# Moving old-key probabilities of all four row tiles, and one chunk of new keys, through square transposes and DRAM in a gated attention block

## The reference, cut to what matters

```
x = layernorm(x)                       # 4 x 512 x 512
q = x @ wq.T ; k_new = x @ wk.T ; v_new = x @ wv.T
k = concat([ctx, k_new])               # 1024 keys
v = concat([ctx, v_new])
attn = softmax(q @ k.T / sqrt(512))    # 512 x 1024 a batch
out = (attn @ v) @ wo.T
x = x + tanh(g_xattn) * out
x = x + tanh(g_ffn) * relu(layernorm(x) @ sign(up).T * up_scale) @ sign(down).T * down_scale * output_scale
```

## Time and profile before

| | us |
|---|---|
| median of 3 runs | 582.67 |
| the profiled execution | 583.08 |
| span of its instructions | 581.1 |
| TensorE busy in it | 575.6 |
| VectorE, ScalarE, GpSimd busy | 392.0, 280.6, 117.8 |

### The profile page before, as it was taken

The page is one execution under the profiler, slowest core; times in us unless marked ns, Lnnn a source line. Parts: engine busy times, 40 slices in busy tenths (PEclk is TensorE's granted clock), DMA queues, the critical chain, the costliest instruction groups (busy, mean ns, idle before and its releaser), DMA issues.

```text
span 581.1 us, 6945 instructions
## 1 busy us (share of the span) xinstructions
PE 575.6 (99%) x2642; PEld 478.5 (82%) x2642; DVE 392.0 (67%) x552; ACT 280.6 (48%) x406; POOL 117.8 (20%) x111
## 2 busy tenths in 40 slices
PE   9999999999999999999999999999999999999997
PEld 7888888888888888888888888888888888888885
DVE  5889554587675587673587676777569644766654
ACT  3783522473322463322475455656458345555531
POOL 5006403003003003003002015242422012332002
PEclk9999999999999999999999999999999999999999
DMA  8714432024115055115124613283821311230011
GB/s 288 241 70 138 81 108 73 18 70 130 38 46 99 16 202 145 38 50 97 33 76 109 216 49 133 74 180 109 177 78 37 144 32 42 95 123 37 0 73 72
DMA packets 76352, 55.78 MB, mean 96 GB/s; under 512 B 54944, under 2 KB 59040, under 8 KB 75936
## 3 DMA queue, kind: packets, MB, share of 16 engines
q1 hardware_dynamic: 76320, 55.34, 32.4%
HBM read 42.74 MB, written 12.60 MB: 95 GB/s over the span
## 4 chain that ended last, share of the span: by engine, by line
PE 98%; DVE 1%; ACT 0%; issue 0%
PE proj L673 36%; PE score L791 19%; PE turn L776 12%; PE score L706 9%; PE score L673 7%; PE proj L776 5%; PE proj L706 4%; PE score L916 2%; PE turn L665 1%; PE score L665 1%; PE score L923 1%; DVE rows L1775 1%; DVE scaled L1772 0%; ACT four_x L1008 0%; PE proj L665 0%; ACT weights L1000 0%
## 5 line engine op out<-in xcount | busy, mean ns | idle before, releaser
L791 PE MATMUL score<-down_signs,hid_split 128*128 128x512 f32 x512 | 133.4, 389 | 0.0
L791 PEld LDWEIGHTS score<-down_signs,hid_split 128*128 128x128 f32 x512 | 96.0, 188 | 20.3 <-DVE hid_split L1656 0.5
L673 PE MATMUL proj<-probsT,four_x 128*128 128x512 f32 x384 | 88.1, 390 | 0.0
L673 PEld LDWEIGHTS proj<-probsT,four_x 128*128 128x128 f32 x384 | 71.8, 188 | 14.7
L673 PE MATMUL proj<-four_x,weights 128*128 128x512 f32 x336 | 76.8, 389 | 0.0
L673 PEld LDWEIGHTS proj<-four_x,weights 128*128 128x128 f32 x336 | 63.0, 188 | 13.0
L597 POOL TENSOR_TENSOR four_x<-raw_ctx,four_x 128x2048 fp32r<-128x2048 f32 x7 | 32.6, 4656 | 147.9 <-ACT four_x L1004 147.9
L1656 DVE TENSOR_TENSOR hid_split<-hid,hid_split 128x512 fp32r<-128x512 f32 x64 | 44.3, 695 | 15.5 <-ACT hid_split L1218 15.4
L776 PE MATMUL turn<-ops_b,up_ops 128*128 128x512 f32 x192 | 51.3, 389 | 0.0
L1012 ACT ACTIVATE four_x<-proj 128x512 fp32r<-128x512 f32 x32 | 19.0, 593 | 65.4 <-PE proj L673 65.4
L1218 ACT ACTIVATE hid_split<-hid 128x512 fp32r<-128x512 f32 x64 | 40.0, 630 | 20.9 <-PE score L791 18.1
(11 more groups left out here) (136 smaller groups left out, 861.1 us busy)
## 6 DMA issues: line engine op xcount, KB each, us to landing
raw_w<-in_ffn_w SPq DMA_DIRECT2D x21, 512.0 KB, 3.3
raw_ctx<-in_ctx_turned SPq DMA_DIRECT2D x4, 1024.0 KB, 5.3
raw_ctx<-in_ctx SPq DMA_DIRECT2D x4, 1024.0 KB, 5.3
raw_x<-block_rows SPq DMA_DIRECT2D x4, 1024.0 KB, 6.0
result<-rows SPq DMA_DIRECT2D x16, 256.0 KB, 2.0
rows<-in_x SPq DMA_DIRECT2D x3, 1024.0 KB, 8.2
turned_x<-in_x_turned SPq DMA_DIRECT2D x3, 1024.0 KB, 5.3
probs_rows<-probs_squares SPq DMA_DIRECT2D x32, 64.0 KB, 2.3
```

What stands on the lines that cost most here:

```text
L673: last = pe.matmul(bank, lhs(l), rhs(r), start=start and i == 0, stop=stop and i == 2)
L791: last = pe.matmul(wide(r), hid_split[:, n % HR, s, r * P:(r + 1) * P], down_signs[:, chunk_of(q), :], start=(q == 0 and s == HI), stop=(q ...
```

## The change

Four things. The old half of all four tiles and the first of the four new chunks (640 columns in all, `FAR = 5` chunks of 128) go through the squares; TensorE turns three new chunks a tile, in four jobs a batch, and no late turn is left. The squares are stored tile by tile (16 DMAs a batch, 8 before) and read back in two halves, tiles 2 and 3, then 0 and 1, each with its own semaphore, copy and subtraction. The values product leads with the three turned new chunks of all four e (36 matmuls; e = 2 and 3 accumulate in the `turn` banks), waits once for both halves, and then adds five chunks to each e. On VectorE `norm_turned` stands ahead of the output of e = 0 in every batch; the second half's subtraction stands behind the block statistics.

```diff
-    TURNS_BATCH = 2 * RT - 2
+    TURNS_BATCH = RT
...
+        FAR = RT + 1
+        PAIRS = ((2, 3), (0, 1))
+        probs_squares = at("probs_squares", 160, [P, RT, FAR * P])
...
             def place_squares(b):
-                for k, t in enumerate(SQUARED):
-                    sp.wait_ge(probs_squared, len(SQUARED) * b + k + 1)
-                    for i in range(P // SQ):
-                        sp.dma_start(probs_squares_v[b, k, i], probs_squares[i * SQ:(i + 1) * SQ, k].rearrange(
-                            "n (j a) -> n j a", a=SQ)).then_inc(probs_out_done, 16)
+                for h, pair in enumerate(PAIRS):
+                    for t in pair:
+                        sp.wait_ge(probs_squared, tile_done(b, t))
+                        for i in range(P // SQ):
+                            sp.dma_start(probs_squares_v[b, t, i], probs_squares[i * SQ:(i + 1) * SQ, t].rearrange(
+                                "n (j a) -> n j a", a=SQ)).then_inc(squares_stored[h], 16)
                 sp.wait_ge(scored, product_scored(b, A22, 1))
-                for k, t in enumerate(SQUARED):
-                    sp.wait_ge(probs_out_done, STORED * len(SQUARED) * (b + 1))
-                    sp.dma_start(squares_placed[:, 0:RT, t * P:(t + 1) * P], probs_rows_v[b, k]).then_inc(placed, 16)
+                for h, pair in enumerate(PAIRS):
+                    sp.wait_ge(squares_stored[h], 2 * STORED * (b + 1))
+                    cols = slice(pair[0] * P, (pair[1] + 1) * P)
+                    sp.dma_start(squares_placed[placed_part(h)], probs_rows_v[b][:, :, cols]).then_inc(placed[h], 16)
...
             # TensorE, values product
-                for e, side in ((0, NEW), (1, NEW), (0, OLD), (1, OLD), (2, NEW), (2, OLD), (3, NEW), (3, OLD)):
...
+                for e in range(DC):
+                    if e == 1:
+                        pe.wait_ge(proj_lo, values_out(b, 3))
+                    for i, (lhs, rhs) in enumerate(new_terms(e)):
+                        if e == 0:
+                            pe.wait_ge(proj_lo, values_out(b, max(i + FAR - RT, 2)))
+                        last = product(proj_bank(n + DC + e), lhs, rhs, i == 0, False)
+                pe.wait_ge(placed_lo, 2 * b + 2)
+                pe.wait_ge(ctx_ready, values_split(b) + 1)
+                for e in range(DC):
+                    for i, (lhs, rhs) in enumerate(old_terms(e)):
+                        last = product(proj_bank(n + DC + e), lhs, rhs, False, i == FAR - 1)
                     last.then_inc(proj_done, 1)
...
             # ScalarE
-            def placed_out(b):
-                act.wait_ge(placed, 16 * len(SQUARED) * (b + 1))
-                act.activation(probsT[:, HI][PLACED], squares_placed[PLACED], ACT.Copy).then_inc(placed_hi, 1)
+            def placed_out(b, h):
+                act.wait_ge(placed[h], 16 * (b + 1))
+                part = placed_part(h)
+                if h == 0:
+                    act.wait_ge(squares_stored[1], 2 * STORED * (b + 1))
+                act.activation(probsT[:, HI][part], squares_placed[part], ACT.Copy).then_inc(placed_hi, 1)
...
             # VectorE, batch(b)
-                square_probs(b, 0)
+                square_probs(b, 2)
                 maxima(b, 0)
-                square_probs(b, 1)
+                square_probs(b, 3)
                 sum_scores(b, AT_C12, 1)
                 maxima(b, 1)
+                square_probs(b, 0)
                 proj_out(b, 0, chunk(new_side, 0))
...
+                square_probs(b, 1)
                 proj_out(b, 1, chunk(new_side, 1))
...
-                for i in range(RT, TURNS_BATCH):
-                    probs_out(b, i)
-                placed_low(b)
+                placed_low(b, 0)
                 dve.wait_ge(exp_done, RT * b + RT)
...
+                placed_low(b, 1)
...
                 else:
+                    norm_turned(b + 1)
                     for e in range(DC):
                         proj_out(b, DC + e, chunk(qT, e))
-
-                        if e == (1 if b == 0 else 0):
-                            norm_turned(b + 1)
-                        if e == (2 if b == 0 else 1):
+                        if e == 0:
                             next_rows_low(b + 1)
-                        if e == 2 and b >= 1:
+                        if e == 1 and b >= 1:
                             turn_pair_squares(b - 1)
```

More of the change, by code:

```diff
@@ L227, in turn_bank, with turned_cols @@
             return turn[:, n % 4, :] if n % 4 < 2 else score[1][:, n % 4 - 2, :]
+        def turned_cols(n):
+            return 4 * P if n < RT else KEYS - FAR * P
         def proj_bank(n):
-            return wide(n) if n < DC else proj[:, n % 2, :]
+            if n < DC:
+                return wide(n)
+            i = (n - PROJS_FIRST) % PROJS_BATCH
+            return turn[:, i - 6, :] if n >= PROJS_FIRST and i in (6, 7) else proj[:, n % 2, :]
         small_in, ctx_in, out_stored = map(sem, ("small_in", "ctx_in", "out_stored"))
@@ L668, in cols @@
             def cols(src):
-                return [src[:, k * P:(k + 1) * P] for k in range(4)]
+                return [src[:, k * P:(k + 1) * P] for k in range(src.shape[1] // P)]
             def product(bank, lhs, rhs, start, stop):
@@ L688, in v_terms, with new_terms, old_terms @@
                 return [(out_of(xT, c, r * P, (r + 1) * P), out_of(weights[:, W_V], c, 0, DIM)) for c in range(DC)]
[L690 to L693, removed]
+            def new_terms(e):
+                return [(out_of(new_side, r, e * P, (e + 1) * P), out_of(probsT, RT + r, 0, ROWS))
+                        for r in range(FAR - RT, RT)]
+            def old_terms(e):
+                side = [(ctx_side, r) for r in range(RT)] + [(new_side, r) for r in range(FAR - RT)]
+                return [(out_of(buf, r, e * P, (e + 1) * P), out_of(probsT, k, 0, ROWS))
+                        for k, (buf, r) in enumerate(side)]
             def score_bank(i, t):
@@ L1007, in turn_out @@
                 act.wait_ge(turned, n + 1)
-                act.activation(dst, four(turn_bank(n)), ACT.Copy).then_inc(turn_hi, 1)
+                act.activation(dst, four(turn_bank(n)[:, 0:turned_cols(n)]), ACT.Copy).then_inc(turn_hi, 1)
             def proj_out(n, dst):
@@ L1378, in probs_out, with square_probs, placed_low @@
             def probs_out(b, i):
-                t, side = TURN_ORDER[i]
-                turn_out(turn0(b) + i, lambda s: probsT[:, s, 4 * side:4 * side + 4, t * P:(t + 1) * P])
-            def square_probs(b, k):
-                dve.wait_ge(exp_done, tile_done(b, SQUARED[k]))
-                if k == 0:
-                    dve.wait_ge(scored, product_scored(b, S2, 1))
-                dve.transpose(probs_squares[:, k, :], probs[:, SQUARED[k], 0:ROWS]).then_inc(probs_squared, 1)
-            def placed_low(b):
-                dve.wait_ge(placed_hi, b + 1)
-                dve.tensor_tensor(probsT[:, LO][PLACED], squares_placed[PLACED], probsT[:, HI][PLACED].bitcast(F32),
+                t = TILE_ORDER[i]
+                turn_out(turn0(b) + i, lambda s: probsT[:, s, FAR:KC, t * P:(t + 1) * P])
+            def square_probs(b, t):
+                dve.wait_ge(exp_done, tile_done(b, t))
+                if t == TILE_ORDER[0]:
+                    dve.wait_ge(scored, product_scored(b, S1, 1))
+                dve.transpose(probs_squares[:, t, :], probs[:, t, 0:FAR * P]).then_inc(probs_squared, 1)
+            def placed_low(b, h):
+                dve.wait_ge(placed_hi, 2 * b + h + 1)
+                part = placed_part(h)
+                dve.tensor_tensor(probsT[:, LO][part], squares_placed[part], probsT[:, HI][part].bitcast(F32),
                                   ALU.subtract).then_inc(placed_lo, 1)
```

62 lines of the change are left out of this document (20 added, 42 removed).

## The result

The changed kernel takes 599.63 us (595.78 to 603.9, six runs) against 582.62 for the kernel before: a ratio of 1.0294 [1.0251, 1.0337]. The forecast was 585.4, and the range, 581.0 to 589.0, doesn't hold it. The profiled execution took 595.78, with a span of 592.8; the other executions granted TensorE a mean clock of 0.979 to 0.990, this one 0.994. The clock turns out to be a part of the loss. Of the 12.7 us between the two profiled executions 11.7 lie in the spans; the other 1.0 lies outside (3.0 beyond the span here, 2.0 before) and has no row.

The account below looks back on a forecast made before the run. TensorE, with 98% of the chain, was taken as the bound. First batch +3.0 (-1.3 transposes, +2.0 squares, +2.3 facts) and -0.3 for the other three gave +2.7 us: 585.4, range 581.0 to 589.0.

Parts of the forecast that it names:

- the transposes' worth: On TensorE, 12 of 24 transposes go per batch at 0.109 us each: 1.31 us a batch, 5.24 over four.
- the due time: Squares are due on TensorE 20.4 us after the value rows start: 159.4 in the second batch, 72.4 in the first.
- the chain and its order: Path of the squares: SP stores, first read, ScalarE copy, VectorE subtraction, gain, block statistics, second subtraction; TensorE stands 1.2 us.
- the release by VectorE's second subtraction: TensorE's gaps ahead of the values product's fourth part, some 2 us first batch, 1.2 others, end with this subtraction.
- statistics between the halves: VectorE's block statistics and moments, 2.88 us, delay the second subtraction; without them it would be 1.4 ahead of due.
- The sign: Whole kernel forecast slower, by 2.7 us; chance of slower by more than 0.2% was 0.62.
- the facts' stand: First batch, ahead of the output projection: TensorE waits for late row facts behind `norm_turned`, 2.3 us.
- The stands: TensorE waits for the squares in the values product: 2.0 us in the first batch, 1.2 in each other.
- 640 KB about 3.8: Read of squares, 640 KB, takes about 3.8 us, between 512 KB in 3.3 and 1024 KB in 5.3.
- the even spacing of 0.56: SP's sixteen stores of squares start 0.56 us apart, taken between 0.52 before and 0.65 by pieces.
- Rival 4: TensorE's clock falls while it stands, in the first batch: 3 us or so more, 588.5; chance 0.03.
- stores paced at 0.65: Rival for SP's stores: cost goes by pieces, first read 1.4 us later in every batch, 590.6; chance 0.12.

Follow-up runs that it names:

- f4_all: Changed kernel with four chunks in squares, first-batch row load behind the squares, its norm behind the second output, relaxed up-product waits, VectorE reordered: 581.05 us, 0.9969.
- a_all: Changed kernel, five chunks kept, with statistics behind the second subtraction, first-batch row load behind squares, norm behind second output, up product's wait relaxed: 584.22 us, 1.0031.
- a_again: The changed kernel run once more, nothing altered: 597.49 us, 1.0255 against the kernel before.
- b_stand: The kernel before, with TensorE made to wait for five small GpSimd powers in each batch, nothing else moved: 602.32 us, 1.0345.
- a_facts: Changed kernel, but in the first batch SP issues the row facts' store only when both reads of squares have landed: 601.84 us, once.
- f4_late: Changed kernel with four chunks in squares, not five, and the first batch's load of the next rows issued behind the squares: 583.53 us, 1.0017.
- a_late_stats: Changed kernel with block statistics behind the second subtraction and the first batch's load of turned rows behind the squares: 587.95 us, 1.0085.
- f4_fin: f4_all with T4's high part moved behind ScalarE's copy of the first up product: 581.42 us, 0.9982.

## Why the prediction was wrong

Right: the transposes' worth (0.109 each, as f4_all's first batch shows), the due time within 0.55 (20.93 for 20.4), the chain and its order, the release by VectorE's second subtraction, and that statistics between the halves are on the path. The sign followed from these.

Wrong were two terms of the squares' chain (1 and 2), the clock (3) and the facts' stand (4):

1. **The stands were 2.0 to 4.1 and not 1.2 to 2.0** (12.2 in all for 5.6, and 2.2 in the leads). Two terms of the chain were too small, by about the same over the four batches. The first is the read, "640 KB about 3.8", worked out between 512 KB in 3.3 and 1024 KB in 5.3. The read on the path took 4.91, 5.05 and 4.30 in the later batches and 5.24 in the first, 4.3 beyond the forecast in all. The rows used were loads of whole rows. The squares' read takes pieces of 1 KB that were written a moment before, and the nearest row was the squares' own, 256 KB in 3.1, which is already as long as a whole-row load of twice its size; I gave it the wrong neighbours. f4_all's page has 512 KB in 4.1. What draws such a read out no run separates: its pieces, the fresh data, or the second read, which is issued 1.5 behind the first (the DMA engines' share is 1.00 from 156.26 to 159.76, while both are under way). That last rival was not tried.
2. **The stores.** The second term is the even spacing of 0.56. Steady stores were 0.586 apart (0.54 and a gap of 0.04), which gives 0.4 by the sixteenth; and in three of four batches one store was longer (1.80, 1.29, 1.97). Before, only the first batch had such a store (2.37, and again 2.27 now), and the forecast gave it to that batch alone. First reads were issued at +15.0, +10.7, +11.4 and +12.4 from the start of the value rows, where +14.0 and three times +10.4 were forecast. With the second read of the first batch, issued 1.2 late, the later batches' 0.3, 1.05 and 2.0 make 4.5. Why single stores are long stays open.

```profile
240.89 1.29 SPq L461
...
244.01 5.05 DMA squares_placed<-probs_rows
...
329.30 1.97 SPq L461
...
334.25 4.30 DMA squares_placed<-probs_rows
```

3. **Rival 4 had 0.03.** "The waits I forecast are shorter, and by that it stays" was the argument. But the clock fell behind stands of 1.96 (a_all), 2.55 and 2.74 (a_again) and of 3.3 (b_stand, all four). It didn't behind 2.03, 2.94 and 3.12 (the profiled execution), 2.13 (a_again), 2.08 and 2.99 (a_facts); of the stands of 3.3 and more none was spared. That is three of nine between 1.96 and 3.12, and ten of ten from 3.3 on. The Trainium skill ("TensorE: Matmul & The Clock Gate", HAM oscillation) names gaps of more than about 3.4 us; the runs show falls behind shorter ones, and the measurement decides. The price, "3 us or so" for one fall, was not low: 1.4 to 2.25 (what the products behind a fall took beyond their time with a restart). What was low is the number of falls: one in the profiled execution, three in a_again's, four in b_stand's. The profiled execution had one fall and the median lies 3.9 above it; two or three more would do it, but of the other executions there is only the mean clock, 0.979 to 0.990 for 0.994.
4. **The facts' stand of 2.3 was 0.** VectorE's wait was there (6.73 us for `all_facts`, ended at 83.17), but the values product had been put back by the first stand and covered it. Two waits in a row don't add when the first delays what the second is due for. In f4_late, without the first, it came to 2.5, near the forecast's figure. So the 0 here is the other error's doing and no merit of the sum.

```profile
83.17 2.29 DVE L1443 TENSOR_TENSOR turned_x<-turned_x,all_facts 128x2048 f32<-128x2048 f32 x1 [6.73 <-DMA all_facts<-row_facts]
```

In the forecast's own sum, -5.24 + 5.6 + 2.3 = +2.7 becomes -5.24 + 12.2 + 2.2 + 0.6 + 0 = +9.8, and the clock adds 2.25 in the mildest execution; by their mean clocks it adds more in the others.

The range failed with the terms: it allowed for one thing at a time, stores paced at 0.65 (590.6, already outside it) or one fall of the clock (588.5), and here stores, reads and clock came late together, in several batches.

## What to carry to other kernels

When a chain of DMAs is lengthened, take the time of a read from the same kind of read (the same pieces, data just written, the same company on the queue), not from the size alone, and allow for a long issue among the stores. Where TensorE would have to stand, count each stand of about 2 us or more as its length and some 1.4 to 2.3 us on top, with a chance (it was 3 of 9 up to 3.1 us and 10 of 10 from 3.3 on); in this kernel the version with fewer transposes removed and no stand at the squares (f4_all) was worth more than the one that removed more. A wait that is hidden by another comes out once that one is repaired, so look for the next before giving a figure.

## What the runs showed of the hardware

- A stand of 3.3 us brought the clock down four times out of four (b_stand), for 1.5 to 1.6 us each; shorter ones did in some executions and not in others.
- In the first batch the facts' store of 4 KB, scattered in elements of 4 bytes, took 9.9 us until its follower could start in the changed kernel, 10.6 with nothing beside it (a_facts: 0 GB/s between 75 and 84), and 12.6 and 13.3 where 1 MB was issued just ahead of it (f4_late, a_late_stats).
- Some VectorE instructions were slow ahead of the last stage, where GpSimd works beside it (busy for 1.17 us of 344 to 346, 7.84 of 346 to 354). Two rows of the same line and shape in f4_fin:

```profile
344.36 1.22 DVE L1515 TENSOR_TENSOR ops_a<-raw_x,ops_a 128x1024 fp32r<-128x1024 f32 x1
...
347.18 1.76 DVE L1515 TENSOR_TENSOR ops_a<-raw_x,ops_a 128x1024 fp32r<-128x1024 f32 x1
```

The kernel before has such rows too (1.75 at 347.78, for 1.23 at 345.50). It may be why handing a copy from one engine to the next only moved the wait there. That GpSimd is the cause was not tried by itself, and one row doesn't fit: at 351.14 the same shape took 1.21 while GpSimd was at work.
